# Second attention: middle products, contexts and key folds as 64-row tiles side by side, and the sixth projection ahead of the second outer products

## What is computed

```
q_hk = (hidden_q @ Wq.T).reshape(Bv, Sv, H, K)            # H=16 heads, K=128
q_big = einsum('bshk,hkq->bshq', q_hk, w_kc_q)            # q: 192
q_big = _apply_rope(q_big, sin_q, cos_q)
kv_r = _apply_rope(kv_c, sin_k, cos_k)                    # 64 wide
q_r = einsum('bshq,hqr->bhsr', q_big, W_qr)               # r: 64
k_r = einsum('bld,hdr->bhlr', kv_r, W_kr)
attn = softmax(einsum('bhsr,bhlr->bhsl', q_r, k_r))
ctx_c = einsum('bhsl,bld->bhsd', attn, kv_r)
ctx_lat = einsum('bhsd,hkd->bhsk', ctx_c, w_kc_kv)
return (ctx_lat as H*K columns) @ Wo.T
```

## Time and profile before

| | us |
|---|---|
| median of 3 runs | 555.42 (554.33 to 555.51) |
| the profiled execution, its own time | 551.76 |
| its span, first to last instruction | 549.2 |
| TensorE busy with matmuls | 400.2 |
| VectorE busy | 378.7 |
| ScalarE busy | 228.4 |
| GpSimd busy | 129.8 |

### The profile page before, as it was taken

One profiled execution on the slowest core, in us unless ns is written; L12 is line 12 of the kernel. 1 busy time (PEld: TensorE's weight loads), 2 busy tenths in 40 slices (PEclk: granted clock), 3 DMA queues, 4 the chain that ended last, 5 costly groups with the idle time before them and its releaser, 6 DMA issues.

```text
span 549.2 us, 10989 instructions
## 1 busy us (share of the span) xinstructions
PE 400.2 (73%) x3620; PEld 278.6 (51%) x3627; DVE 378.7 (69%) x919; ACT 228.4 (42%) x473; POOL 129.8 (24%) x135
## 2 busy tenths in 40 slices
PE   2647757551466666405999999999999999927892
PEld 1435545551233333304567575766757498815672
DVE  5998998958698998477475758566575744772441
ACT  2767898540488877403113132231313222124440
POOL 1090000001455553200000000192000049343232
PEclk9977897865788878856999999999999999958997
DMA  8944650310112221155041330402000080323000
GB/s 322 404 166 166 217 227 2 122 40 29 37 59 59 58 53 42 39 153 162 0 133 45 89 128 4 131 0 74 0 0 1 10 317 1 134 77 97 30 31 19
DMA packets 17621, 50.56 MB, mean 92 GB/s; under 512 B 2248, under 2 KB 6480, under 8 KB 16560
## 3 DMA queue, kind: packets, MB, share of 16 engines
q1 hardware_dynamic: 14640, 42.19, 22.1%
q0 software_dynamic: 2944, 7.88, 5.2%
HBM read 43.25 MB, written 6.82 MB: 91 GB/s over the span
## 4 chain that ended last, share of the span: by engine, by line
PE 51%; DVE 33%; issue 8%; DMA 3%; ACT 2%; DVEq 1%; POOL 1%; SPq 0%; ACTq 0%; POOLq 0%
PE bank L850 13%; PE bank L1057 7%; PE bank L859 6%; PE bank L947 5%; PE bank L865 4%; DVE mx L1345 4%; PE bank L906 3%; DVE raw L1384 3%; DVE hs L1513 3%; DVE hid L1510 2%; PE bank L795 2%; PE bank L782 2%; DVE hid L1511 2%; PE bank L886 2%; DVE W L1394 2%
## 5 line engine op out<-in xcount | busy, mean ns | idle before, releaser
L1556 DVE TENSOR_TENSOR roped<-bank,cst 128x512 f32<-128x512 f32 x96 | 61.8, 686 | 45.1 <-PE bank L850 43.6
L566 POOL TENSOR_TENSOR WE<-WE,wT 128x512 f32<-128x512 f32 x32 | 40.4, 1300 | 196.8 <-DMA WE<-_L_ffn_expert_masks_dram 123.5
L546 POOL DMA_INDIRECT xg<-x_rows,owner_b x24 | 23.6, 982 | 116.1 <-DVE owner_b L391 93.6
L1210 ACT ACTIVATE prob<-prob 128x512 f32<-128x512 f32 x16 | 10.0, 632 | 76.4 <-DVE prob L1565 76.4
L850 PE MATMUL bank<-XNT_hi,AW_hi 128*128 128x512 f32 x96 | 41.5, 432 | 0.3
L850 PE MATMUL bank<-XNT_hi,AW_lo 128*128 128x512 f32 x96 | 37.9, 395 | 0.0
L850 PE MATMUL bank<-XNT_lo,AW_hi 128*128 128x512 f32 x96 | 37.8, 393 | 0.0
L859 PE MATMUL bank<-roped,MW 128*64 128x512 f32 x128 | 31.0, 605 | 0.1
L947 PE MATMUL bank<-VW,ctxT 128*128 128x256 f32 x128 | 30.8, 386 | 0.0
L756 PE MATMUL bank<-W,xgT 128*128 x90 | 28.4, 443 | 2.8 <-issue 1.8
L553 POOL DMA_INDIRECT y_rows<-y,slot x24 | 24.1, 1005 | 25.6 <-ACT y L1171 22.6
(11 more groups left out here) (290 smaller groups left out, 966.9 us busy)
## 6 DMA issues: line engine op xcount, KB each, us to landing
raw<-in_L_ffn_w_dram SPq DMA_DIRECT2D x8, 1536.0 KB, 6.7
f_all<-in_L_xattn_fold_dram SPq DMA_DIRECT2D x8, 768.0 KB, 5.3
kv<-in_keys_values_dram SPq DMA_DIRECT2D x8, 656.0 KB, 7.7
WE<-_L_ffn_expert_masks_dram SPq DMA_DIRECT2D x5, 768.0 KB, 8.1
WE<-_L_ffn_expert_masks_dram SPq DMA_DIRECT2D x3, 1024.0 KB, 8.7
yg<-y_rows SPq DMA_DIRECT2D x8, 256.0 KB, 5.0
x_tok<-pay SPq DMA_DIRECT2D x8, 256.0 KB, 2.2
f_rot<-in_L_xattn_rot_dram SPq DMA_DIRECT2D x8, 224.0 KB, 6.3
```

What stands on the lines that cost most here:

```text
L546: pool.indirect_dma_start(out=xg[j % 4][:].bitcast(U32), out_offset=None, in_=x_rows, in_offset=bass.IndirectOffsetOnAxis(ap=RB.owner[:, j ...
L566: pool.tensor_tensor(WE[:, e], WE[:, e], wT[:], ALU.mult).then_inc(WE_ready, 1)
L1556: ins = dve.tensor_tensor(roped[n][:, r, :].rearrange("p (b s) -> p b s", s=S), src, cst[:, None, at:at + S].to_broadcast([P, 8, S]), ALU. ...
```

## The change

- **Middle products.** `to_keys_middle` no longer takes g. For each r it issues four matmuls of 64 x 64 with 512 columns, one for each head and token half, which leave out the zero blocks of `MW`. To put the four on different tiles, the output halves of the two heads are swapped in token half 1 (`half(h, g)`), in the outer products and in `qrT` too. The semaphore `keyed` goes up by 2 at the end of all, instead of by 1 after each half.
- **Order.** Projection 4 now comes ahead of the first outer products and projection 5 ahead of the second.
- **Contexts and scores.** Odd batch rows have the heads swapped (`place_of`), so the contexts use all four 64 x 64 tiles. Because the tiles' banks change halfway, `scores` and `contexts` each have a `settle` in their middle: the last matmul raises a semaphore and PE waits for it itself.
- **Key folds.** `W_qr`'s parts for r = 0 and 1 lie on partitions 0 to 63 and 64 to 127 (with `W_kr` on both), and the two results go to two banks, of which bank 1 is one that projections write. The wait for the masked product moves from behind projection 3 to behind projection 0. DVE masks the two halves with one instruction each. A load of `f_rot` becomes 128 x 512 elements instead of 64 x 896.
- **The key fold of unit 0** moves from behind the second last block of the first FFN to behind the wait for the last one's copy.
- Four semaphores are merged into two, which frees one for `settle`.

```diff
-R_W = 4 * QD + P
+R_W = 2 * QD + P
+M_BANKS, M_BANKS_0 = (3, 1), (3, 2)
...
-        f_rot = [sb(f"f_rot{i}", [S, R_W]) for i in range(2)]
+        f_rot = [sb(f"f_rot{i}", [P, R_W]) for i in range(2)]
...
-            def fold_keys(u, par):
-                for r in range(2):
-                    for c, (at, n) in enumerate(((0, 64), (64, 128), (192, 64))):
-                        k0 = 64 if c == 2 else 0
-                        mm = pe.matmul(bank[3][:, r * 2 * P + at:r * 2 * P + at + n],
-                                       f_rot[par][:, r * 2 * QD + c * P:r * 2 * QD + (c + 1) * P],
-                                       f_rot[par][:, 4 * QD + k0:4 * QD + k0 + n], start=True, stop=True)
+            def fold_keys(u, par, banks=M_BANKS):
+                for c, (at, n) in enumerate(((0, 64), (64, 128), (192, 64))):
+                    k0 = 2 * QD + (64 if c == 2 else 0)
+                    for r in range(2):
+                        mm = pe.matmul(bank[banks[r]][:, at:at + n], f_rot[par][r * S:(r + 1) * S, c * P:(c + 1) * P],
+                                       f_rot[par][r * S:(r + 1) * S, k0:k0 + n], start=True, stop=True)
                 mm.then_inc(M_ready, 1)
...
                     fold_values(0, 0, V_BANK_0)
-                if j == NBLK - 2:
-                    fold_keys(0, 0)
             pe.sem_inc(keyed, 2)
             pe.sem_inc(s_ready, 1)
             pe.sem_inc(c_ready, 1)
             pe.wait_ge(y_copied, NBLK + 1)
+            fold_keys(0, 0, M_BANKS_0)
+            def half(h, g):
+                return h if g == 0 else 1 - h
+            def place_of(h, b):
+                return h if b % 2 == 0 else 1 - h
+            def settle(mm, n):
+                mm.then_inc(first_half, 1)
+                pe.wait_ge(first_half, n)
+                pe.sem_inc(pe_waited, 1)
...
                         for h, n, at in ((0, g, 0), (1, 2 + g, 192)):
-                            pe.matmul(bank[2 + g][h * S:(h + 1) * S, :], MW[par][:, r, at:at + S], roped[n][:, r, :],
+                            pe.matmul(bank[2 + g][half(h, g) * S:(half(h, g) + 1) * S, :], MW[par][:, r, at:at + S], roped[n][:, r, :],
                                       start=r == 0, stop=False, skip_group_check=True)
-                def to_keys_middle(g):
-                    pe.wait_ge(roped_ready, NUNIT * u + 4 + g + 3)
+                def to_keys_middle():
+                    pe.wait_ge(roped_ready, NUNIT * u + NUNIT + 2)
+                    pe.sem_inc(pe_waited, 1)
                     for r in range(2):
-                        mm = pe.matmul(bank[2 + g][:], MW[par][:, r, 64:192], roped[4 + g][:, r, :],
-                                       start=False, stop=r == 1, skip_group_check=True)
-                    mm.then_inc(keyed, 1)
-                for n in range(4):
+                        for g in range(2):
+                            for h in range(2):
+                                at, to = h * S, half(h, g) * S
+                                mm = pe.matmul(bank[2 + g][to:to + S, :], MW[par][at:at + S, r, S + at:2 * S + at], roped[4 + g][at:at + S, r, :],
+                                               start=False, stop=r == 1, skip_group_check=True)
+                    mm.then_inc(keyed, 2)
+                project(0)
+                pe.wait_ge(M_done, u + 1)
+                for n in range(1, 4):
                     project(n)
                 pe.wait_ge(V_done, u + 1)
-                pe.wait_ge(M_done, u + 1)
+                project(4)
                 to_keys_outer(0)
-                project(4)
+                project(5)
                 to_keys_outer(1)
-                project(5)
-                to_keys_middle(0)
-                to_keys_middle(1)
+                to_keys_middle()
...
                 for b in range(2 * NT):
+                    if b == NT:
+                        settle(mm, 2 * u if not isinstance(u, int) or u else 1)
                     for h in range(2):
-                        mm = pe.matmul(bank[4 + h][64 * (b % 2):64 * (b % 2) + 64, (b // 2) * S:(b // 2 + 1) * S],
-                                       qrT[h * S:(h + 1) * S, b * S:(b + 1) * S], kvrT[h * S:(h + 1) * S, b * S:(b + 1) * S],
+                        at = half(h, b // NT) * S
+                        mm = pe.matmul(bank[4 + place_of(h, b)][64 * (b % 2):64 * (b % 2) + 64, (b // 2) * S:(b // 2 + 1) * S],
+                                       qrT[at:at + S, b * S:(b + 1) * S], kvrT[at:at + S, b * S:(b + 1) * S],
                                        start=True, stop=True)
...
-                for n in range(2 * NT):
-                    for h in range(2):
-                        b = (n + NT * h) % (2 * NT)
-                        mm = pe.matmul(bank[6 + b // NT][h * S:(h + 1) * S, (b % NT) * S:(b % NT + 1) * S], kvr2[h * S:(h + 1) * S, b, :],
-                                       probT[h * S:(h + 1) * S, b * S:(b + 1) * S], start=True, stop=True)
+                for n in range(NT):
+                    if n == NT // 2:
+                        settle(mm, 2 * u + (3 if not isinstance(u, int) or u < NU - 1 else 2))
+                    lo, hi = (0, NT) if n < NT // 2 else (NT, 0)
+                    for h, b in ((0, lo + 2 * (n % 4)), (1, hi + 2 * (n % 4)), (0, hi + 2 * (n % 4) + 1), (1, lo + 2 * (n % 4) + 1)):
+                        at = place_of(h, b) * S
+                        mm = pe.matmul(bank[6 + b // NT][h * S:(h + 1) * S, (b % NT) * S:(b % NT + 1) * S], kvr2[at:at + S, b, :],
+                                       probT[at:at + S, b * S:(b + 1) * S], start=True, stop=True)
...
                 dve.wait_ge(M_ready, u + 1)
-                dve.tensor_tensor(MW[par][:], bank[3][:].rearrange("p (r n) -> p r n", r=2),
-                                  mask_m[:, None, :].to_broadcast([P, 2, 2 * P]), ALU.mult).then_inc(M_done, 1)
+                for r in range(2):
+                    ins = dve.tensor_tensor(MW[par][:, r, :], bank[m_banks[r]][:, 0:2 * P], mask_m[:], ALU.mult)
+                ins.then_inc(M_done, 1)
...
     qr = np.asarray(w_qr).reshape(NU, 2, 2, QD // 2, S).transpose(0, 4, 1, 2, 3)
-    both = np.stack([qr, qr[:, :, :, ::-1]], axis=2).reshape(NU, S, 4 * QD)
-    return np.concatenate([both, np.asarray(w_kr).reshape(NU, P, S).transpose(0, 2, 1)], axis=2)
+    both = np.stack([qr, qr[:, :, :, ::-1]], axis=1).reshape(NU, P, 2 * QD)
+    keys = np.asarray(w_kr).reshape(NU, P, S).transpose(0, 2, 1)
+    return np.concatenate([both, np.concatenate([keys, keys], axis=1)], axis=2)
```

More of the change, by code:

```diff
@@ L332, in build @@
         prob_turned, probT_ready, c_ready, ctxT_ready = (sem(n) for n in ("prob_turned", "probT_ready", "c_ready", "ctxT_ready"))
-        o_ready, x3_ready, pe_waited = sem("o_ready"), sem("x3_ready"), sem("pe_waited")
+        o_ready, x3_ready, pe_waited, first_half = sem("o_ready"), sem("x3_ready"), sem("pe_waited"), sem("first_half")
         m_loaded = [sem(f"m_loaded{i}") for i in range(3)]
@@ L338, in build @@
         scales_ready, l_summed, centred, x_tok_stored = (sem(n) for n in ("scales_ready", "l_summed", "centred", "x_tok_stored"))
-        pairs_ready, spots_d_ready, owner_d_summed, owner_d_ready = (
-            sem(n) for n in ("pairs_ready", "spots_d_ready", "owner_d_summed", "owner_d_ready"))
-        s_parts_ready, s_summed = sem("s_parts_ready"), sem("s_summed")
+        pairs_ready, one_hots_ready, one_hots_summed, owner_d_ready = (
+            sem(n) for n in ("pairs_ready", "one_hots_ready", "one_hots_summed", "owner_d_ready"))
         var_ready, root_ready = sem("var_ready"), sem("root_ready")
@@ L1011, in _ @@
             count_d(7)
-            pe.wait_ge(spots_d_ready, 1)
+            pe.wait_ge(one_hots_ready, 1)
             for t in range(NT):
@@ L1016, in _ @@
                                    start=t == 0 and part == 1, stop=t == NT - 1 and part == 2)
-            mm.then_inc(owner_d_summed, 1)
+            mm.then_inc(one_hots_summed, 1)
             def turn_rows_d(b):
@@ L1027, in sort_scales @@
             def sort_scales():
-                pe.wait_ge(s_parts_ready, 1)
+                pe.wait_ge(one_hots_ready, 2)
                 for t in range(NT):
@@ L1031, in sort_scales @@
                                    start=t == 0, stop=t == NT - 1)
-                mm.then_inc(s_summed, 1)
+                mm.then_inc(one_hots_summed, 1)
             def blocks_of(g):
@@ L1538, in _, with fold @@
             dve.sem_inc(s_less, 4)
-            def fold(u, par, banks=A_BANKS):
+            def fold(u, par, banks=A_BANKS, m_banks=M_BANKS):
                 for c in range(2):
@@ L1571, in by_sum @@
                 dve.tensor_tensor(prob[:, :, h, :], prob[:, :, h, :], s_stat[:, h, 2, :, None].to_broadcast([P, NT, S]), ALU.mult).then_inc(prob_ready, 1)
-            fold(0, 0, A_BANKS_0)
+            fold(0, 0, A_BANKS_0, M_BANKS_0)
             for t in range(NT):
@@ L1689, in _ @@
```

(10 more changed lines are left out.)

## The result

The changed kernel takes 535.12 us (534.40 to 536.89) against 555.46 us for the kernel before beside it: a ratio of 0.9651, 95% interval 0.9627 to 0.9674, or 20.3 us less between the medians and 19.4 by the ratio. Measured again next to other kernels it is 0.9646 (0.9623 to 0.9668). The forecast was 538.2 us with a range of 533 to 546; the time is inside, and 3.1 us better than the forecast. Its profiled execution took 536.89 us, with a span of 534.4.

A forecast was written before the change was run, and what follows sets the result against it. TensorE (PE) was taken to bound the second attention. Terms of -12.5 (six loop units), -1.4, -1.5, -0.5 and -1.3 summed to -17.2 us: 534.6 from the profiled execution, 538.2 from the median, range 533 to 546.

The forecast's parts named there:

- M: Middle products of each attention unit (two heads) on four tiles: 3.43 to 1.87 us, net saving 1.46.
- Rival (a): The middle products' four 512-column tiles do not run four at a time, the second pair queues: 550.7 us; chance 0.09.
- Order: Projections 4 and 5 (P4, P5) ahead of outer products (O0, O1): cost 0, middle products fit with 0.3 us to spare.
- Rival (d): DVE or ACT becomes the bound of a unit; a stall of 0.5 us in each gives 542 us; chance 0.11.
- V after Q: PE piece V behind the query fold waits for both query copies, which start only after all middle products: +0.15 us.
- K: Key fold, 1.48 us and bound by weight loads; rotations on two row halves make it 0.80, saving 0.68.
- Rival (b): Weight loads bind: the key fold gains nothing and contexts only half, returning 7.9 us: 546 us; chance 0.11.
- S and C, drains: Scores and contexts each get a drain of 0.40 us; contexts on four tiles take 0.98 without it, saving 0.89.
- Rival (c): Dearer drains: at 1.63 us each all gain is gone, at 1.75 the kernel takes 557 us; chance 0.03.
- Unit in the loop: One loop unit of the second attention: -2.08 us, 23.79 to about 21.7; six units give -12.5.
- Unit 0, unit 7, C(7): Second attention's first unit, last unit and last contexts, outside the six loop units: -1.4, -1.5 and -0.49 us.
- K of unit 0: Tail of the first FFN: the last block's turn no longer waits for the key fold, -1.3 us.

The follow-up runs named there:

- mid_only: Kernel before with only the middle products on four tiles, projections 4 and 5 reordered, swapped halves and the drain in the scores: ratio 0.9853.
- old_order: Changed kernel with projections 4 and 5 back behind the first and second outer products: 0.9906 of the kernel before, 14.4 us slower than the changed kernel.
- settle3: Changed kernel with three drains instead of one in each scores and contexts: 0.9898 of the kernel before, 14.0 us slower than the changed kernel.
- interleaved: Changed kernel with halves of scores and contexts alternating, so each drain has other matmuls in front of it: 0.9597 of the kernel before.
- k0_only: Kernel before with only unit 0's key fold moved behind the wait for the last block's copy in the first FFN: ratio 0.9985.
- hoisted: Changed kernel with the register load of the last three blocks' expert placed ahead of the second product of the block before: 0.9656 of the kernel before.
- ctx_only: Kernel before with only heads swapped on odd batch rows and contexts on four tiles with a drain in their middle: ratio 0.9930.
- layout_only: Kernel before with the new key-fold layout, load, banks, masking and earlier wait, but the fold's six matmuls in the old order: ratio 0.9936.

## Why the prediction was right, point by point

- **Bound.** Right: all pieces of a unit are PE's before and after, at clock 1.00, and what PE saves in a unit the unit saves.
- **M.** Forecast 3.43 to 1.87, measured 1.88. A tile-shape change was put at 0.1 in all and cost 0.20 in front of the query fold (1.50 against 1.30), with nothing in front of M. In the trace this is the fold's first weight load, 0.19 us: before, it started 0.43 us ahead of the fold's first matmul (412.86 and 413.29), and now it starts with it (401.78). Net -1.35 instead of -1.46. Rival (a) is refuted by mid_only.
- **Order.** Right: P4 to O1 lost nothing, and rope 5 ended 0.54 us before M, where 0.3 was forecast. Without the order 1.46 us are lost in each unit (old_order). Rival (d) did not come.
- **V after Q.** Forecast +0.15, measured 0: V keeps its 0.58 or 0.59. The two copies take 1.08 us together and end at 403.00, 0.35 ahead of V's start; I had put 1.34, though the earlier trace rows has 1.08 for two such copies. Even without Q's extra 0.20 they would have ended 0.15 us ahead of V.
- **K.** Forecast 0.80, measured 0.81. It was bound by its weight loads, as the forecast had it, one every 0.11 us. Waiting for the mask behind P0 costs nothing: the rows show the projections going on unbroken. Rival (b) is refuted for K and C.
- **S and C, drains.** 0.40 forecast, 0.41 in the scores (1.50 against 1.09) and 0.40 by settle3. Contexts 1.35 us with the drain, forecast 1.38. Rival (c), 1.63 us a drain, is far off. The high end for a drain rested on 0.54 us as the longest pause; the same chain has one of 0.65 in front of a matmul, which changes nothing at 0.40 measured. The rate of four tiles reaches 14.7 ns a record (0.47 for 32) in the interleaved kernel. The Trainium skill, "TensorE: Matmul & The Clock Gate", section "Wait — 56ns, not 53.3ns?", says that matmuls never start closer together than about 25 ns. The trace does not agree for small matmuls on different tiles.
- **Unit in the loop.** -2.08 forecast; 23.79 to 21.63 measured, -2.16.
- **Unit 0, unit 7, C(7).** From the first P of unit 0 to that of unit 1, 20.99 us became 19.39 (258.53 to 277.92), -1.6 against -1.4. Unit 7 up to the output projection went from 21.64 to 19.61, -2.0 against -1.5: rope 5 ends earlier than I had summed. There the drain and the faster contexts nearly cancelled (4.05 to 3.95 us for T, S and C), as forecast. C(7) went from 2.01 to 1.50 us, -0.51 against -0.49.
- **K of unit 0.** The term with the least behind it. "the turn of the last block (227.66) no longer waits 1.48 us" was forecast as -1.3. Against the profile that the forecast was made from, it is -0.3 (-0.5 in k0_only). ACT's last two copies of turned tiles (hidT) start 2.55 us apart, where they were 3.23 apart and the forecast's 1.3 makes it 1.92, and the product behind them takes 1.05 us instead of 0.67. Two things were put at nothing. The fold had covered a register load for the last block's expert, 0.53 us that nothing covers once it is gone, as hoisted shows by moving it. And the turns and the product behind it ran at half the clock, 0.60 and 1.05 us instead of 0.34 and 0.67. The fold alone does not hold the clock up: of six profiles with the fold in its old place, five show that product at 1.04 or 1.05 us, and only that of the kernel before shows 0.67. Against two of those profiles (mid_only and ctx_only), in which the fold itself ran at half the clock, the changed kernel saves 2.5 us there. So -1.3 lies between the two values that the profiles give, and not for a reason that the forecast had.
- **The total.** The unit, and with it some 15 of the 17.2 us, came as forecast and for the reasons given. Adding up, the forecast -17.2 less what the fold of unit 0 did not give against the same profile is -16.2; the ratios say -19.4 to -19.6. Behind the stretch all profiles spend 106.1 to 107.5 us, so by elimination the other 3 us lie ahead of it. Part of it can be the fold of unit 0 at the lower clock: the forecast's profile was an untypical execution, which at 551.76 us is faster than every other time of that kernel on record (551.79 us and up), and the fold ran at full clock in it. With 2.5 us for the fold the sum is -18.4. Against this stands k0_only, whose interval ends at -2.1 us. What lies still further ahead is code that the change does not touch. The changed kernel was profiled twice and every other one once, so how often the fold runs at the lower clock is not known, and this stays open. The 3.7 us that the forecast added to get from that profile to the median are no constant either: the changed kernel's profiled execution is 1.8 us above its median. That the whole came within 3.1 us is in this part luck.

## What to carry to other kernels

When 64-row products stand in a queue that bounds the kernel, count records per tile before and after: here four tiles ran at twice the rate of two, at 64 columns (15 against 29 ns a record) and at 512 (0.12 against 0.23 us). Merging halves of a product moves a dependency to the earliest point, so the order around it has to be moved with it, or it eats the gain (13 to 14 us here). Where a drain is needed between two phases of one tile set, put another matmul group in front of the wait: the drain of 0.4 us then costs nothing (a unit went from 21.63 to 20.79 us with two drains covered).

## What the runs showed of the hardware

- PE waiting for its own matmul costs 0.40 us at 64 columns (settle3: 1.60 us for four more in a unit).
- Going from 64x64 tiles back to 128x128 cost 0.20 us in front of the query fold, where the first weight load (0.19 us) no longer ran ahead. From 128x64 to 128x128 it was about 0.1 (projection 5 took 1.60 us, a quarter of P0 to P3 1.51).
- Weight loads of 128 columns on one half of the rows followed each other 0.11 us apart (before). Alternating between the two halves, a fold of twelve fell from 1.48 to 0.81 us, and with first one half and then the other to 1.09 (layout_only), since the second half's loads were taken ahead.
- The same fold of twelve took 1.48 us at the 2.4 GHz level and 2.75 at 1.2 GHz (before and mid_only).
- With a register load on PE's queue between a product and the next matmul, a pause of 0.52 to 0.74 us stood in front of that matmul in four profiles. Where the product itself ran at half the clock, 0.14 and 0.33 us were left of it.
